# Feed-forward of a decoder layer on one core: where the shared products stand among logits, tiles and read back

## The reference

```python
x = x + ffn(_layernorm(x))
# ffn, for t = 4096 tokens, 16 experts, one expert per token
logits = hidden @ router_w.T
top_vals, top_idx = jax.lax.top_k(logits, 1)
scores = sigmoid(scatter(top_vals))            # zero off the chosen expert
routed_in = hidden[None, :, :] * scores.T[:, :, None]
gate, up = split(einsum('nth,nhf->ntf', routed_in, gate_up_proj))
expert_sum = einsum('ntf,nfh->nth', up * silu(gate), down_proj).sum(axis=0)
shared = silu(hidden @ shared_gate_w.T) * (hidden @ shared_up_w.T) @ shared_down_w.T
return shared + expert_sum
```

## Time and profile before

| What | us |
| --- | --- |
| median of 3 runs | 513.48 |
| lowest and highest | 512.52, 515.56 |
| the profiled execution's own time | 517.45 |
| its span, first to last instruction | 515.6 |

### The profile page before, as it was taken

The page is one execution under the profiler, slowest core; times in us unless marked ns, Lnnn a source line. Parts: engine busy times, 40 slices in busy tenths (PEclk is TensorE's granted clock), DMA queues, the critical chain, the costliest instruction groups (busy, mean ns, idle before and its releaser), DMA issues.

```text
span 515.6 us, 10998 instructions
## 1 busy us (share of the span) xinstructions
PE 429.5 (83%) x3804; PEld 322.7 (63%) x3804; DVE 298.8 (58%) x886; ACT 263.1 (51%) x603; POOL 201.7 (39%) x280
## 2 busy tenths in 40 slices
PE   2788888777777389999998999799999998888890
PEld 1466566554444268888888887595566666767650
DVE  4777877632665667787877773725733332444434
ACT  5465555347777417777776777424722222333320
POOL 1322222214886626455552000000377501777730
PEclk9999999987888759999998999857999997999996
DMA  6830000001899967667771000000051103788629
GB/s 207 298 97 1 0 0 1 1 0 53 240 259 278 330 160 189 170 180 181 187 198 44 7 4 5 2 0 0 17 175 52 47 1 83 223 286 273 217 63 294
DMA packets 50353, 62.21 MB, mean 121 GB/s; under 512 B 7316, under 2 KB 46772, under 8 KB 48692
## 3 DMA queue, kind: packets, MB, share of 16 engines
q1 hardware_dynamic: 38528, 37.89, 25.1%
q0 software_dynamic: 4864, 20.43, 14.3%
q10 hardware_dynamic: 6912, 3.25, 2.6%
HBM read 43.68 MB, written 20.73 MB: 125 GB/s over the span
## 4 chain that ended last, share of the span: by engine, by line
PE 54%; DVE 15%; ACT 9%; issue 8%; DMA 7%; SPq 5%; ACTq 1%; POOL 0%; DVEq 0%; POOLq 0%
PE bank L709 6%; PE bank L698 5%; PE bank L1234 5%; PE bank L1235 5%; PE bank L1224 4%; PE bank L671 3%; PE bank L1279 3%; DVE mx L778 2%; PE bank L1218 2%; PE bank L733 2%; PE bank L410 2%; PE bank L434 2%; DMA qparts<-qpart 2%; PE bank L397 2%; ACT t_hT L1159 1%
## 5 line engine op out<-in xcount | busy, mean ns | idle before, releaser
L867 ACT ACTIVATE prob<-bank 77x512 f32<-77x512 f32 x128 | 74.3, 595 | 23.4 <-PE bank L698 23.3
L778 DVE TENSOR_REDUCE mx<-bank 128x5 f32<-128x385 f32 (+1 forms) x96 | 54.9, 576 | 18.7 <-PE bank L671 16.0
L1202 POOL DMA_INDIRECT sorted_in<-h_rows,pos_s x32 | 31.5, 986 | 85.9 <-DVE pos_s L1054 76.5
L1207 POOL DMA_INDIRECT routed<-t_y,t_no x48 | 46.4, 966 | 40.8 <-DVE t_y L1092 31.1
L698 PE MATMUL bank<-qst,kst 99*77 99x128 bf16 x512 | 51.0, 223 | 0.2 <-ACT prob L867 0.2
L698 PEld LDWEIGHTS bank<-qst,kst 99*77 99x77 bf16 x512 | 39.2, 117 | 7.8 <-ACT prob L867 3.9
L377 POOL TENSOR_TENSOR qkv<-qkv,rn 128x256 f32<-128x256 f32 x32 | 19.1, 629 | 63.4 <-DVE rn L296 63.4
L1008 DVE TENSOR_TENSOR act<-bank,s_g 128x512 f32<-128x512 f32 x28 | 19.3, 691 | 42.1 <-ACT s_g L1147 42.0
L671 PE MATMUL bank<-kst,qst 96*128 96x77 bf16 x512 | 36.2, 208 | 7.3 <-DVE mx L778 3.7
L1147 ACT ACTIVATE s_g<-bank 128x512 f32<-128x512 f32 x28 | 16.7, 597 | 48.6 <-PE bank L1235 48.6
L1224 PEld LDWEIGHTS bank<-sd,act 128*128 128x128 f32 x224 | 29.2, 192 | 14.9 <-issue 12.3
(11 more groups left out here) (167 smaller groups left out, 1033.3 us busy)
## 6 DMA issues: line engine op xcount, KB each, us to landing
qst<-qparts POOLq DMA_DIRECT2D x36, 256.0 KB, 3.5
t_w<-in_expert_w SPq DMA_DIRECT2D x48, 192.0 KB
qparts<-qpart SPq DMA_DIRECT2D x16, 384.0 KB, 7.7
kst<-kparts POOLq DMA_DIRECT2D x36, 154.0 KB, 3.9
kparts<-kpart SPq DMA_DIRECT2D x16, 231.0 KB, 7.9
sorted_in<-in_fill SPq DMA_DIRECT2D x1, 3168.0 KB, 13.4
t_row<-sorted_in ACTq DMA_DIRECT2D x48, 66.0 KB
qst<-qparts SPq DMA_DIRECT2D x12, 256.0 KB, 6.5
```

What stands on the lines that cost most here:

```text
L778: v.tensor_reduce(mx[:, b % JA, h0:h1], bank[n % 2][:, 0:(h1 - h0) * KEYS].rearrange("p (h k) -> p h k", k=KEYS), AX.X, ALU.max, negate=Tr ...
L867: a.activation(prob[n % PROBS][:].rearrange("p c t -> p (c t)"), bank[2 + n % 2][0:KEYS], ACT.Exp, scale=SCORE_SCALE).then_inc(s["expd"], 1)
L1202: p.indirect_dma_start(out=sorted_in, out_offset=bass.IndirectOffsetOnAxis(ap=pos[:, b:b + 1].bitcast(U32), axis=0), in_=h_rows[:, b], in_ ...
L1207: p.indirect_dma_start(out=routed, out_offset=bass.IndirectOffsetOnAxis(ap=t_no[r][:].bitcast(U32), axis=0), in_=t_y[r][:], in_offset=None ...
```

## The change

The products stand elsewhere; what is computed is the same.

- **Group 0.** Its four chunks' gates and ups go into the logits stage as eight half chunks: one product of 512 columns behind each group's logits (half_chunk). The first two, and the logits of groups 0 and 1, stand in the last steps of the cross attention. VectorE's normalisations are spread between the attention's last additions, and deviation3(a, 1) comes behind copy_h(2) rather than copy_h(0). Its downs stand behind the logits, the count products behind the second of them.
- **Six groups ahead of the tiles** in place of seven.
- **Three chunks of group 6 among the tiles:** gate and up ahead of the down of tiles 14, 28 and 42 (MIXED), their downs ahead of the down of tiles 16, 30 and 44; five chunks behind (one ahead of the last tile's down, as before, and four after it).
- **47 tiles** in place of 48.
- **Read back in long runs:** a token's row of routed is at p * 32 + b, so a partition's eight sequences of one transfer are 4096 bytes in a row. The 32 rows per sequence scaled by ScalarE go out four to a chunk over eight chunks (five over seven before).
- VectorE's final adds (add_routed) stand between the last multiplies, each group with its own store; the fill of onesf moves to GpSimd.

The downs of a shared chunk stand ahead of the down of a tile. The diff, cut to its core:

```diff
-    TILES = TOK // P + EXPERTS
+    TILES = (TOK + EXPERTS * (P - 1)) // P
...
             turn_h(pe, 0)
+            turn_h(pe, 1)
+            logits(pe, 0)
+            half_chunk(pe, 0)
             turn_back(B - 1)
-            turn_h(pe, 1)
+            turn_h(pe, 2)
+            logits(pe, 1)
+            half_chunk(pe, 1)
             project(B - 1)
...
             inverse_root(v, 0)
             normalise3(v, 0)
+            normalise3(v, 1)
             add_attention(B - 2)
             divide(B - 1)
             statistics(B - 2)
             aggregate(B - 3)
-            normalise3(v, 1)
+            normalise3(v, 2)
+            aggregate(B - 2)
+            normalise3(v, 3)
             add_attention(B - 1)
-            aggregate(B - 2)
-            wait_on_copy(v, s["x2"], B)
+            normalise3(v, 4)
+            v.wait_ge(s["x2"], B)
             statistics(B - 1)
+            normalise3(v, 5)
             aggregate(B - 1)
-            v.memset(onesf[:], 1.0)
-            for g in range(2, NG - 1):
-                normalise3(v, g)
+            normalise3(v, 6)
             inverse_root(v, 1)
             normalise3(v, NG - 1)
...
             copy_back(B - 2)
+            copy_h(a, 0)
+            copy_h(a, 1)
             copy_back(B - 1)
-            copy_h(a, 0)
+            copy_h(a, 2)
             deviation3(a, 1)
...
+        def logits(pe, g):
+            pe.wait_ge(s["hT"], g + 1)
+            for b in range(g * JP, (g + 1) * JP):
+                m = pe.matmul(bank[BK_LG][:, b * EXPERTS:(b + 1) * EXPERTS], xT[:, b * P:(b + 1) * P], rw[:], start=True, stop=True)
+            m.then_inc(s["lgp"], 1)
+
+        def half_chunk(pe, i):
+            c = i // 2
+            if i % 2 == 0:
+                if c >= 2:
+                    pe.wait_ge(s["act"], c - 1)
+                pe.matmul(bank[BK_GATE[c % 2]][:], sg[:, c * P:(c + 1) * P], xT[:, 0:GT], start=True, stop=True)
+            else:
+                pe.matmul(bank[BK_UP[c % 2]][:], su[:, c * P:(c + 1) * P], xT[:, 0:GT], start=True, stop=True).then_inc(s["gup"], 1)
 
         def bc(ap, n):
 
...
+            for c in range(CH - 1):
+                gated(0, c)
...
             v.tensor_tensor(oh3, wrk3, bc(low[:], EXPERTS), ALU.is_equal).then_inc(s["oh"], 1)
-            gated(0, 0)
...
             v.reciprocal(posf[:], esc[:]).then_inc(s["sc_ready"], 1)
-            gated(0, 1)
+            gated(0, 3)
...
             v.wait_ge(s["rankp"], 1)
+            v.wait_ge(s["h_kept"], 1)
...
             step(v.tensor_tensor(tot[:], cum[:], bank[BK_COUNT][:], ALU.subtract))
-            gated(0, 2)
...
-            gated(0, 3)
+            gated(1, 1)
+            add_down(0, 0)
...
-            gated(1, 0)
+            gated(1, 2)
...
+            gated(1, 3)
+            for g in range(2, AHEAD_OF_TILES):
+                for c in range(CH):
+                    gated(g, c)
+                    if c == 1:
+                        add_down(g - 1, (g - 1) % 2)
+            add_down(AHEAD_OF_TILES - 1, (AHEAD_OF_TILES - 1) % 2)
...
+            def add_routed(g):
+                if g % 2 == 0:
+                    v.wait_ge(y_in[g // 2], 16)
+                v.wait_ge(s["x3"], max(g + 1, AHEAD_OF_TILES))
+                v.tensor_tensor(xs[:, g * JP:(g + 1) * JP], xs[:, g * JP:(g + 1) * JP], seqs(y_back[g // 2], g % 2), ALU.add).then_inc(s["res_add"], 1)
...
                 leave(n, r, k)
+                if n - 1 in MIXED:
+                    behind_gated(MIXED[n - 1])
...
+            behind_gated(3)
+            behind_gated(4)
+            behind_add(6)
+            behind_gated(5)
+            add_routed(0)
+            add_routed(1)
+            behind_gated(6)
+            add_routed(2)
+            add_routed(3)
+            behind_gated(7)
+            add_routed(4)
+            add_routed(5)
+            behind_add(7)
+            add_routed(6)
+            add_routed(7)
...
+        BK_GATE, BK_UP, BK_DOWN = (0, 6), (2, 5), (3, 4)
+        BK_RANK, BK_COUNT = 7, 1
+        SCALED = B // (2 * CH)
+        AHEAD_OF_TILES = 6
+        BASE = AHEAD_OF_TILES * CH
+        BEHIND = (NG - AHEAD_OF_TILES) * CH
+        MIXED = {14: 0, 28: 1, 42: 2}
+        BEHIND_DOWN = (5, 4)
...
+            for g in range(AHEAD_OF_TILES):
+                body(g, g % 2)
...
-            for g in range(1, NG):
+            def silu(m, gate, gup):
+                a.wait_ge(s["gup"], gup)
+                if gup > 2:
+                    a.wait_ge(s["act"], gup - 2)
+                a.activation(s_g[m % 2][:], bank[gate][:], ACT.Silu).then_inc(s["silu"], 1)
+
+            def scaled_rows(n):
+                for b in range(n * SCALED, (n + 1) * SCALED):
+                    a.activation(h_rows[:, b, 0:D], h_rows[:, b, 0:D], ACT.Copy, scale=posf[:, b:b + 1]).then_inc(s["rows"], 1)
+
+            for g in range(3, NG):
                 copy_h(a, g)
+                if g % 2 == 1:
+                    c = (g - 3) // 2
+                    silu(c, BK_GATE[c % 2], c + 1)
             a.wait_ge(s["lg"], 1)
             a.activation(score[:], best[:], ACT.Exp, scale=-1.0).then_inc(s["escore"], 1)
+            silu(CH - 1, BK_GATE[(CH - 1) % 2], CH)
+            a.wait_ge(s["sc_ready"], 1)
 
...
+                    if n >= CH:
+                        if n - CH < 2 * CH:
+                            scaled_rows(n - CH)
+                        silu(c, BK_GATE[c % 2], n + 1)
...
+                if n in MIXED:
+                    behind_silu(MIXED[n])
...
+            p.memset(onesf[:], 1.0)
...
+            for g in range(2, NG):
+                if g + 1 < NG:
+                    turn_h(pe, g + 1)
+                logits(pe, g)
+                half_chunk(pe, g)
...
-                    if not (first and c < 2):
+                    if g > 0:
                         pe.wait_ge(s["act"], g * CH + (c - 1))
...
+                    if c > 0:
+                        down(g, par, c - 1)
+                    elif g > 0:
+                        down(g - 1, 1 - par, CH - 1)
+                    if g == 0 and c == 2:
...
+            def behind_gate_up(m):
+                pe.wait_ge(s["act"], BASE + (m if m <= len(MIXED) else m - 1))
+                gate, up = behind_banks(m)
+                g, c = AHEAD_OF_TILES + m // CH, m % CH
+                pe.matmul(bank[gate][:], sg[:, c * P:(c + 1) * P], xT[:, g * GT:(g + 1) * GT], start=True, stop=True)
...
+            def behind_down(m):
+                c = m % CH
+                pe.wait_ge(s["act"], BASE + m + 1)
...
                     turn(n + 2, (r + 2) % RING, (n + 2) // RING)
+                if n in MIXED:
+                    behind_gate_up(MIXED[n])
+                if n - 2 in MIXED:
+                    behind_down(MIXED[n - 2])
                 if last_tile(n, 1):
-                    last_gate_up(0)
+                    behind_gate_up(len(MIXED))
...
+            pe.wait_ge(s["tact"], TILES)
+            pe.wait_ge(s["ty"], TILES)
+            for m in range(len(MIXED) + 1, BEHIND):
+                behind_gate_up(m)
+                behind_down(m - 1)
+            behind_down(BEHIND - 1)
...
-                    sp.dma_start(y_back[g // 2][:], routed[g * GT:(g + 2) * GT].rearrange("(j p) f -> p j f", p=P)).then_inc(y_in[g // 2], 16)
+                    sp.dma_start(y_back[g // 2][:], routed[0:TOK].rearrange("(p b) f -> p b f", p=P)[:, g * JP:(g + 2) * JP]).then_inc(y_in[g // 2], 16)
...
-    second += [(np.arange(B)[None, :] * P + r[:, None]).astype(np.int32).view(f32)]
+    second += [(r[:, None] * B + np.arange(B)[None, :]).astype(np.int32).view(f32)]
```

## The result

The changed kernel takes **495.85 us** (median of 4 executions, 492.99 to 496.79) against 513.73 us before in the same comparison (512.52 to 515.56). The ratio is 0.964, with a 95% interval of 0.959 to 0.969: faster by 17.9 us, where 7.6 us were forecast. The profiled execution has a span of 493.4 us, 22.2 less than before's 515.6, but before's profiled run lay 3.7 us above its own median.

What follows compares the result with a forecast made beforehand. TensorE was taken to bound the kernel up to tile 0, partly at half clock, GpSimd the tile stage, then a tail. Terms 418.3 + 10.4 + 60.1 + 19.2 = 508.0 us span, so 505.9 us; range 496.5 to 511.5.

Steps and rivals of the forecast that it cites:

- Step 1: Logits stage with the half chunks: logits complete at 347.1 us with the clock held, about 353.7 with it fallen, the choice taken.
- that copy: ScalarE's copy of group 3 in the logits stage, behind the last four sequences' deviation; TensorE to wait about 1.7 us.
- The judgement on the clock: Logits stage: TensorE's clock falls in the new 1.7 us wait at 336 to 338 us.
- the held case: Rival: the clock holds through the logits stage; logits at 347.1, first copy at 410.2, 497.8 us in all; chance 0.36.
- The fall itself: Logits stage: with the clock down, four groups run at 4.17 us each, logits at about 353.7 instead of 347.1.
- The reason behind the judgement: Logits stage: transposes and thin products do not engage full clock, leaving only the half chunks to hold it.
- Step 2: Routing, from logits to positions: 15.0 us with the clock held, 16.5 with it down; 17.6 before.
- Step 3: Up to tile 0: scatter and TensorE paths side by side; first copy at 418.3 us, or 410.2 with the clock held.
- The sign given for it: Before tile 0: the last scatter of sorted rows ends at or after TensorE's last down.
- Step 4: Tile stage: 10.4 us to tile 4, then 60.1 to the last scatter, 5.1 longer than before, set by TensorE.
- their small DMA waits: Tile stage: waits included in the 1.22 us per tile taken from tiles 4 to 46 of the kernel before.
- Step 5: Tail from the last scatter to the end: 19.2 us instead of 20.1, with 0.9 gained by the long-run read back.

Runs made afterwards that it cites:

- wait1: The changed kernel with one more 512-column copy on ScalarE ahead of the copy of group 3, its result read by nothing; 500.6 us, ratio to before 0.971.
- before_stream: The kernel before with seven 256-column products, read by nothing, in and behind the wait for the last sequences, no work moved; 506.5 us, ratio 0.986.
- three wait kernels: The changed kernel with one, two or four more ScalarE copies ahead of the copy of group 3; 500.6, 505.9 and 499.2 us.
- before_again: The kernel before, profiled once more with no edit; 515.3 us (one execution).
- wait4: The changed kernel with four more ScalarE copies ahead of the copy of group 3, so TensorE waits 3.04 us; 499.2 us (one execution).
- wait2: The changed kernel with two more ScalarE copies ahead of the copy of group 3, so TensorE waits 2.00 us; 505.9 us (one execution).
- fill_start: The changed kernel with one group 6 chunk moved into TensorE's wait at tile 0 and two instead of three among later tiles; 495.3 us, ratio 0.964.
- after_b: The changed kernel once more, unedited, in a set of runs about 10% slower for every kernel; 542.9 us, ratio to before 0.961.

## Why the prediction was wrong

By its own steps, in the order of the sum; spans of the changed kernel's profile.

**Step 1, the failed step.** The prediction said: "TensorE waits about 1.7 us for that copy" and "I take it that the clock falls there." The copy's wait measured 0.96 us. It was estimated from a deviation "at about 337", 12.8 us after A; it came at 335.92, 12.1 after A, while TensorE was ready for the thin products of group 3 at 335.78, 12.0 after A. The deviation was added up too late in two places: TensorE's moved work delayed VectorE's last addition of the attention by 2.8 us, not 3.0, and the two normalisations added 1.7 us, not 2.2, as they took the place of shorter instructions that stood there before. The judgement on the clock was right for the wait it was made for: with 1.48 us (wait1) the clock fell in three of four executions, with 0.96 it held, by the mean clock in all four. The mis-sized term of 0.7 us turned the sum from one case into the other, worth 8.1 us of the 14.6 us of span between forecast (508.0) and result (493.4). The logits were complete at 346.37 where the held case has 347.1: the difference is that same 0.7 us. (The fall itself was added up a little low: four groups at 4.17 instead of 2.09 us, the last without its half chunk, give 7.5 us and not 6.6.) I gave the held case 0.36; with a wait known to no better than 1 us it deserved about half.

The reason behind the judgement was half wrong. I argued that the rule on transposes "leaves only the half chunks to hold it". That rule is the Trainium skill's (TensorE: Matmul & The Clock Gate, Part 4: PE-mode transpose): transposes do not engage the full clock. before_stream held 1.00 through 8.6 us of transposes and thin products alone. That idle gaps throttle, as the Trainium skill has it in HAM oscillation on the same page, agrees with the three wait kernels, though the gaps here were shorter than the ones it speaks of.

One of the forecast's readings was wrong too: that "the fall came while the engine was busy half the time" takes the mean of 330 to 333 us. TensorE was busy from 329.67 to 331.58 and idle from then on, and the clock was down 0.15 us later.

**Step 2** was right in size: positions 15.5 us after the logits (15.0), at 361.90 (362.1 in the held case).

**Step 3** was right in shape: scatters 41.85 us, and ScalarE's load issues (3.87 us) in front of the first copy, with TensorE's first transpose done at 407.5. The scatter path was the later one by 0.18 us, where 0.7 was forecast for the held case; a tie that could have gone either way. The sign given for it did not show: the last scatter ended at 403.75, ahead of TensorE's last down (407.44), because the path runs through the last silu and not through that down. From the end of the last sorted scatter (403.75) to the first load issue it took 1.35 us, not the 2.3 taken from the median landing. First copy 409.01 against 410.2.

**Step 4** kept its sign and was 3.5 us too dear. The start to tile 4 took 9.2 us instead of 10.4: TensorE was at half clock for 3.4 us here (410.6 to 414.1) and for some 7 us in before (430.7 to 437.5). From tile 4 to the last scatter 57.8 us against 60.1: 41 regular steps at 1.18 instead of 1.22 us (1.8 less), three chunks at 2.55 instead of 2.7 us (0.4 less), the fourth in front of the last down as priced (that step took 1.66 us). The 1.22 held "their small DMA waits" of before; TensorE has no wait for a DMA between 418 and 477 us in the changed kernel's profile; in wait1, with the same code there, it has two, 0.8 us in sum, so part of this is chance of a run. GpSimd idled 3.9 us, 5 were forecast, most of it in the places named: behind tiles 14 to 16, 28 to 30 and 42 to 46. That TensorE sets the end of the stage is thus right.

**Step 5.** The tail is 17.35 us, 19.2 were forecast. The long runs are worth about the 0.9 us that I took for them, though by the stores and not by an earlier first add. The rest is the landing: the read back was issued 2.39 us after the start of the last scatter, and the sum had carried over the 4.23 us of before's profile. So the first add came 6.5 us after the last scatter and not some 8.

Of the whole gain some 7 to 8 us are thus the clock, seen from two sides: some 8 us go when the half chunks leave the stage and the clock falls, and 7.3 us come by filling the waits in the old kernel. The rest is four chunks that no longer stand ahead of tile 0, of which the tile stage gives some back, the four moved into the logits stage, and the tail. The share of single edits in these last 10 us was not separated, because the runs meant for it lay in the slower sets.

## What to carry to other kernels

Where a resource has two levels, the size of the wait that decides between them is the term to work out most carefully: here 0.96 us of wait cost nothing more, and 1.48 us cost 3.6 us. But add up all waits of the stretch and not only the last: in the kernel before the clock was down as its longest wait began. Independent products are best spread into a stage full of waits rather than stood behind it: they do their own work, and here the clock held with them. And a tail read from one execution should be held against a second before it enters a sum: 1.5 us of this one did not come again.

## What the runs showed of the hardware

- Transposes and 16-column products kept a full clock for 8.6 us at a busy share of 1.00 (before_stream), yet did not bring a fallen one back in 16.6 us at the same busy share (before, before_again).
- With the same instructions behind the wait, up to the logits, the clock stayed down for 6.8 us in wait1 and 10.2 us in wait4; in wait2, with the shared products behind them, for 20.5 us.
- In the tile stage a wait of 1.22 us (fill_start) and one of 1.54 us (before_again) each had a fall some 2 us behind it; one of 1.17 us (before_again) and one of 0.98 us (before_stream) had none.
- In three sets of runs, on three chips, every kernel took some 10% longer; on one of these chips the kernel before had taken 514 us minutes before. In the traces of these sets TensorE, ScalarE and VectorE stand still together in the scatter phase, while GpSimd keeps its rhythm of 1.27 us. The rows are the busy times in the stretch 386 to 406 us of after_b, then of the changed kernel, and one row of the waits in 374 to 412 us of after_b (total, times, longest):

```profile
386.00:406.00 20.00, 1.50 (x3) 0.34 (x1) 0.00 (x0) 0.00 (x0) 13.91 (x15) 0.59 0.15 51
```

```profile
386.00:406.00 20.00, 19.76 (x94) 12.63 (x92) 6.50 (x10) 4.78 (x8) 13.55 (x14) 1.00 0.15 51
```

```profile
ACT s_g L1178 <- remote: 34.4, 3, 26.0
```

The trace names no releaser within the core for the 34.4 us of ScalarE's waits. What stops the engines was not found out and stays open; the ratio of the changed kernel to before was the same with it (0.961) as without (0.964).
